# Mixer weights split in place at the mixer's end, and attention scores one slot earlier, in an early-fusion layer on one core

## The reference, cut to what matters

```python
h = s4d(log_dt, x, B, inv_A_real, A_imag, 1024)      # mixer: [16, 128, 1024]
h = concatenate([h, txt], axis=1)                    # [16, 205, 1024], txt has 77 rows

# attention, 32 heads of 32, one key head and one value head for all of them
qkv = layernorm(h) @ Wqkv                            # 1024 -> 1024 + 32 + 32
scores = einsum("bqhd,bkd->bhqk", q, k) * d ** -0.5 + alibi, causal
h = h + einsum("bhqk,bkd->bqhd", softmax(scores), v).reshape(...) @ Wo

# feed-forward: base product, and a rank-16 part of 8 experts by a router
h = h + ffn(layernorm(h))

# in the mixer, for each of 128 channels h and 64 states n
V = exp(dtA[:, :, None] * ell)                       # ell = 0 .. 1023
K = 2.0 * einsum("chn,hnl->chl", Cc, V).real
```

## Time and profile before

| what | us |
|---|---|
| median of 3 runs (1617.25 to 1621.37) | 1620.49 |
| the profiled execution: its time, its span | 1622.69, 1620.9 |
| mixer block, first instruction to the last issue of its loads | 0 to 176.4 |
| attention block until its first projection | 176.9 to 199.1 |
| pair 0; pairs 1 to 6; pair 7; drain | 59.3; 536.9; 89.6; 73.4 |
| MLP block | 958.3 to 1620.9 |

### The profile page before, as it was taken

How to read it: one execution, slowest core, us unless ns; L and a number is a source line. 1 busy time by engine, 2 the same in 40 slices (tenths; PEclk the granted TensorE clock), 3 DMA queues, 4 the chain that set the end, 5 groups by cost and what they waited for, 6 DMA issues and landing times. The chain is left out here.

```text
span 1620.9 us, 28815 instructions
## 1 busy us (share of the span) xinstructions
PE 1464.8 (90%) x9700; PEld 1312.3 (81%) x9700; DVE 1124.5 (69%) x4170; ACT 744.9 (46%) x2642; POOL 399.9 (25%) x289
## 2 busy tenths in 40 slices
PE   0477299999999999999998989999999999999999
PEld 0477298887888888887887768999898989898988
DVE  8996478889898989888888846444453544444454
ACT  4585158686878878786878731110101011110100
POOL 0000124453544445443544501101010101010110
PEclk9877699999999999999999999999999999999999
DMA  7554466465554656464567351121212121111210
GB/s 214 156 131 90 111 103 116 72 105 95 83 113 63 126 84 121 70 116 77 97 152 140 91 206 59 39 79 39 78 39 78 52 65 53 63 65 51 69 48 40
DMA packets 112269, 147.79 MB, mean 91 GB/s; under 512 B 13284, under 2 KB 97636, under 8 KB 111704
## 3 DMA queue, kind: packets, MB, share of 16 engines
q1 hardware_dynamic: 111064, 145.82, 39.5%
q10 hardware_dynamic: 1088, 0.52, 0.2%
HBM read 69.18 MB, written 46.66 MB: 71 GB/s over the span
## 5 line engine op out<-in xcount | busy, mean ns | idle before, releaser
L820 ACT ACTIVATE P<-P,nmax 128x128 f32<-128x128 f32 (+1 forms) x1024 | 434.5, 426 | 96.9 <-DVE nmax L917 93.0
L891 POOL TENSOR_TENSOR P<-P,rden 128x512 f32<-128x512 f32 (+1 forms) x256 | 329.4, 1308 | 419.8 <-DVE rden L923 419.8
L917 DVE CUSTOM_DVE_ANT_0 P<-sc,mask 128x128 f32<-128x128 f32 (+1 forms) x1024 | 292.1, 323 | 70.0 <-PE sc L695 65.3
L725 PE MATMUL pr<-xT_hi,wq_hi 128*128 128x410 f32 x576 | 242.7, 421 | 0.9 <-DVE xT_lo L943 0.9
L929 DVE COPY PTR<-pt 128x282 f32<-128x282 f32 x512 | 220.9, 432 | 17.0 <-PE pt L705 15.9
L1191 PE MATMUL b<-w_hi,x2T_hi 128*128 128x390 f32 (+3 forms) x624 | 214.7, 344 | 1.0 <-DVE x2T_lo L1323 1.0
L1191 PE MATMUL b<-w_lo,x2T_hi 128*128 128x390 f32 (+3 forms) x624 | 212.7, 341 | 0.0
L1191 PE MATMUL b<-w_hi,x2T_lo 128*128 128x390 f32 (+3 forms) x624 | 212.2, 340 | 0.0
L725 PE MATMUL pr<-xT_lo,wq_hi 128*128 128x410 f32 x576 | 201.3, 350 | 0.0
L725 PE MATMUL pr<-xT_hi,wq_lo 128*128 128x410 f32 x576 | 200.5, 348 | 0.0
L1284 POOL TENSOR_TENSOR ht<-ht 128x1024 f32<-128x1024 f32 (+1 forms) x24 | 58.3, 2428 | 575.8 <-DVE ht L1313 575.8
(11 more groups left out here) (187 smaller groups left out, 2946.0 us busy)
## 6 DMA issues: line engine op xcount, KB each, us to landing
Qs<-q_hi SPq DMA_DIRECT2D x128, 205.0 KB, 4.8
ht<-h_dram SPq DMA_DIRECT2D x42, 512.0 KB, 3.6
Qs<-q_lo SPq DMA_DIRECT2D x64, 205.0 KB, 5.7
att_dram<-att SPq DMA_DIRECT2D x64, 205.0 KB, 3.1
at<-att_dram SPq DMA_DIRECT2D x25, 512.0 KB, 4.9
out<-ht SPq DMA_DIRECT2D x23, 512.0 KB, 2.7
h_dram<-Y SPq DMA_DIRECT2D x60, 128.0 KB, 3.1
h_dram<-in_txt SPq DMA_DIRECT2D x1, 4928.0 KB, 26.0
```

Source lines behind the costliest of these rows:

```text
L725: last = nc.tensor.matmul(out, w[a][:, i, cols], xT[x][:, i, :], start=(i == 0 and m == 0), stop=(i == KC - 1 and m == 2))
L820: last = nc.scalar.activation(P[rows, j % 2, i, cols], P[rows, j % 2, i, cols], ACT.Exp, scale=-1.0, bias=nmax[at], accum_out=den[at])
L891: lastp = nc.gpsimd.tensor_tensor(w, w, r, ALU.mult)
L917: lastv = v.tensor_tensor_reduce(P[0:n, j % 2, i, cols], sc[i % 2][0:n, cols], mask[0:n, m], 1.0, 3.0e38, ALU.add, ALU.min, nmax[0:n, j % ...
```

## The change

Mixer. The stage is gone. The weights, now laid out on the host as 128 rows of nine pieces, are copied from the input to a DRAM buffer, and from there three pieces at a time into `wq_lo` itself, all issued in step 0. ACT makes pieces 0 to 4 of `wq_hi` in steps 2 to 6 and pieces 5 to 8 after the last magnitudes; DVE subtracts in place, all nine pieces after the last Q. Step 6 makes Q in quarters too, and the last step's magnitudes wait for them. SP loads the text tiles ahead of the stores of step 6, DVE norms those two tiles in the mixer block, and of the last 8 stores ACT issues 6. Attention: kv is the third projection, q2 the fourth; scores begin one slot earlier; output weights are split from slot 1 on, in turns 4 and 7; `a_lo` is done in halves; at the start DVE norms two tiles and not four; POOL fills its constant rows once they are normalized.

```diff
-    stage = sb("w_stage", [128, 2, DM])
...
+    FINE = LAST - 1
+    Q_PARTS = FINE + 2 * QUARTERS
+    SP_LAST = 2
...
-            load_piece(0)
-            load_piece(1)
-
+            sp.dma_start(io["wqkv_dram"], io["Wqkv"]).then_inc(wqkv_copied, 16)
             sp.dma_start(io["h_dram"].rearrange("(c s) d -> c s d", s=S)[:, CH:S, :], io["txt"]).then_inc(txt_copied, 16)
             for step in range(MIX_STEPS):
-                if step + 2 < PIECES:
-                    load_piece(step + 2)
+                if step == 0:
+                    sp.wait_ge(wqkv_copied, 16)
+                    for n in range(PIECES // 3):
+                        cols = slice(3 * n * DM, (3 * n + 3) * DM)
+                        sp.dma_start(W["wq_lo"][:, cols].bitcast(F32), io["wqkv_dram"][:, cols]).then_inc(w_loaded[n], 16)
...
-                if step == MIX_STEPS - 1:
-                    sp.wait_ge(q_ready, LAST + QUARTERS)
+                if step == FINE:
+                    sp.wait_ge(q_ready, Q_PARTS)
                     for c in range(2):
                         sp.dma_start(W["ht"][0:TXT, 2 * c + 1, :], io["txt"][c]).then_inc(W["h_loaded"][2 * c + 1], 16)
                 sp.wait_ge(y_copied, step + 1)
-                for a in range(AH if step < LAST else AH // 2):
+                for a in range(AH if step < LAST else SP_LAST):
...
-                    act.wait_ge(q_ready, step)
+                    act.wait_ge(q_ready, step if step < LAST else FINE + QUARTERS)
...
             for step in range(MIX_STEPS):
-                if step == LAST:
-                    hi_piece(PIECES - 1)
                 for part in ((wave, magnitudes) if step % 2 == 0 or step == LAST else (magnitudes, wave)):
                     part(step)
-                if step == 0:
-                    hi_piece(0)
-                if step < LAST:
-                    hi_piece(step + 1)
+                if 2 <= step < LAST:
+                    hi_piece(step - 2)
                 if step >= 1:
                     copy_out(step - 1)
+            for k in range(LAST - 2, PIECES):
+                hi_piece(k)
             copy_out(LAST)
...
-                lo_piece(step)
-                if step == LAST:
-                    lo_piece(PIECES - 1)
                 dve.wait_ge(wave_ready, step + 1)
-                for r in range(QUARTERS if step == LAST else 1):
+                for r in range(QUARTERS if step >= FINE else 1):
...
+            for k in range(PIECES):
+                lo_piece(k)
+
+            for c in range(2):
+                dve.wait_ge(W["h_loaded"][2 * c + 1], 16)
+                x = W["ht"][0:TXT, 2 * c + 1, :]
+                free(v.bn_stats(st[0:TXT, c, 0, :], x[:, 0:512]))
+                link(v.bn_stats(st[0:TXT, c, 1, :], x[:, 512:1024]))
+                link(v.bn_aggr(mvt[0:TXT, c, :], st[0:TXT, c].rearrange("p a b -> p (a b)")))
+            link(v.tensor_scalar(ve[0:TXT], mvt[0:TXT, :, 1], EPS, None, ALU.add))
+            for k in range(RSQRT_LINKS):
+                link(rsqrt_step(nc, k, rs[0:TXT], ve[0:TXT], rt[0:TXT]))
+            for c in range(2):
+                x = W["ht"][0:TXT, 2 * c + 1, :]
+                v.tensor_scalar(x, x, mvt[0:TXT, c, 0:1], rs[0:TXT, c:c + 1], ALU.subtract, ALU.mult).then_inc(txt_done, 1)
...
-    MAIN = [("q", 0), ("q", 1), ("q", 2), "kv", ("q", 3), ("q", 4), ("q", 5), ("q", 6), ("q", 7)]
+    MAIN = [("q", 0), ("q", 1), "kv", ("q", 2), ("q", 3), ("q", 4), ("q", 5), ("q", 6), ("q", 7)]
...
-    SCORE_SLOT = [5, 6, 7, 8, 9, 10, 11, 12]
+    SCORE_SLOT = [4, 5, 6, 7, 8, 9, 10, 11]
...
-    SPLIT_AT = [GH * (n + 2) + 2 + 3 * h for n in range(7) for h in range(2)] + [GH * SLOTS + 2 * n for n in range(4)]
+    SPLIT_AT = [GH * (n + 1) + 4 + 3 * h for n in range(WO_PIECES - 1) for h in range(2)] + [GH * SLOTS + 1, GH * SLOTS + 3]
...
-    A_HI_AT, A_LO_AT = [0, 12, 28], [1, 14, 30]
+    A_HI_AT, A_LO_AT = [0, 12, 28], [2, 14, 30]
...
             pool.wait_ge(const_loaded, 32)
+            pool.wait_ge(xn_ready, 4)
...
-            for s in (1, 3, 0, 2):
+            for s in (0, 2):
                 for part in range(3):
                     ln_stats(0, 3 * s + part, link)
             for step in range(RSQRT_LINKS + 1):
                 ln_rstd(step, link)
-            for s in range(4):
-                ln_apply(0, s, link)
+            for s in (0, 2):
+                ln_apply(0, s, link, 2)
```

More of the change, by code:

```diff
@@ L157, in mixer_block @@
     ident_loaded, txt_copied = sem("ident_loaded"), sem("txt_copied")
-    w_loaded = [sem("w_loaded0"), sem("w_loaded1")]
+    w_loaded, wqkv_copied = [sem(f"w_loaded{i}") for i in range(3)], sem("wqkv_copied")
     w_hi, w_lo = sem("w_hi"), sem("w_lo")
@@ L182, in mixer_block @@
     LAST, QUARTERS = MIX_STEPS - 1, 4
+    FINE = LAST - 1
+    Q_PARTS = FINE + 2 * QUARTERS
+    SP_LAST = 2
+    scratch = tab[:, 1].rearrange("p h a -> p (h a)")
+    st = scratch[:, 0:24].rearrange("p (c a b) -> p c a b", c=2, a=2)
+    mvt = scratch[:, 24:28].rearrange("p (c a) -> p c a", c=2)
+    rs, rt, ve = (scratch[:, 28 + 2 * i:30 + 2 * i] for i in range(3))
+    txt_done = sem("txt_done")
     with nc.Block() as block:
@@ L261, in hi_piece @@
             def hi_piece(k):
-                act.wait_ge(w_loaded[k % 2], 64 * (k // 2 + 1))
-                nc.scalar.activation(piece(W["wq_hi"], k), stage[:, k % 2, :], ACT.Copy).then_inc(w_hi, 1)
+                act.wait_ge(w_loaded[k // 3], 16)
+                nc.scalar.activation(piece(W["wq_hi"], k), piece(W["wq_lo"], k).bitcast(F32), ACT.Copy).then_inc(w_hi, 1)
             def copy_out(step):
@@ L415, in _ @@
                 pe.wait_ge(x2_ready, step + 1)
-                if step < LAST:
+                if step < FINE:
                     pe.wait_ge(q_ready, step + 1)
@@ L421, in _ @@
                     out = ps[step % 2 * BANKS_STEP + j // 4][:, j % 4, :]
-                    if step == LAST and j % 4 == 0:
-                        pe.wait_ge(q_ready, step + j // 4 + 1)
+                    if step >= FINE and j % 4 == 0:
+                        pe.wait_ge(q_ready, FINE + (step - FINE) * QUARTERS + j // 4 + 1)
                     for x, first in ((X, True), (X2, False)):
@@ L983, in ln_rstd, with ln_apply @@
                     link.issued(rsqrt_step(nc, step - 1, rstd[:], veps[:], rtmp[:]))
-            def ln_apply(p, s, link):
+            def ln_apply(p, s, link, tiles=1):
                 n = TILES[s][2]
@@ L989, in ln_apply @@
                 v.tensor_scalar(ht[0:n, s, :], ht[0:n, s, :], mv[0:n, s, 0:1], rstd[0:n, s:s + 1],
-                                ALU.subtract, ALU.mult).then_inc(xn_ready, 1)
+                                ALU.subtract, ALU.mult).then_inc(xn_ready, tiles)
             def body(p, first, last):
-                link = Chain(dve, chain, CHAINS * (p + 1) if last is False else 0, const_ready)
+                link = Chain(dve, chain, CHAINS * (p + 1) - TEXT_CHAINS if last is False else 0, const_ready)
                 for slot, main, sj, tj, aj in slots(p, first, last):
@@ L1011, in body @@
                             v.tensor_tensor(lo, half_of(wo_stage(k // 2), k % 2), hi.bitcast(F32), ALU.subtract).then_inc(wo_lo, 1)
-                        if last is None and GH * slot + i in A_LO_AT:
-                            a_lo(A_LO_AT.index(GH * slot + i))
+                        for half in range(2):
+                            if last is None and GH * slot + i - half in A_LO_AT:
+                                a_lo(A_LO_AT.index(GH * slot + i - half), half)
                         if last is None and out_half(slot, i, 1)[1] == KC - 1:
```

51 lines of the change are left out of this document (23 added, 28 removed).

## The result

The changed kernel takes 1611.53 us (1609.54 to 1613.25, 5 runs), the kernel before 1620.06 beside it on the same chip: a ratio of 0.9949, 95% interval 0.9935 to 0.9964. It is faster by 8.5 us where 19.9 were forecast, and inside the range (1588 to 1614), near its upper end.

The account below looks back on a forecast made before the run. DVE was taken to pace the mixer, and PE to be busy nearly throughout the attention slots. Mixer with stores -17.2, start of attention -6.7 and slots +4.0 gave -19.9 us, from 1620.49 to 1600.6; range 1588 to 1614.

Parts of the forecast that it names:

- the size of slot 5: Attention pairs: 7.3 us of work, but q3 lands 9.6 us after slot start, so PE waits about 2 us before slot 6.
- this meeting: Slot 4 of each pair: POOL's scaling begins just before DVE's applies, costing 0.6 us per pair, between 0 and 2.6.
- every meeting with POOL costs the rest of POOL's operation: DVE and POOL share a port pair, so a collision blocks DVE for the rest of POOL's operation, 1.3 us each.
- The rival of a clock that falls behind the wait: Clock falls in each pair near slot 5's wait, losing 3.4 us x 8 = 27: 1628 us, slower; chance 0.08.
- Slot 3: Attention pairs: a slot without scores, where DVE's backlog from slot 2 is worked off; 8.3 us.
- Pair 7: Last attention pair: no norm, and a split half in turn 6 meets DVE's slack; -1.0 us, an estimate.
- The drain: End of attention: one unit less, -4.9 us, and halves of a_lo with two splits fewer, 1.5 us; together -6.4.
- q5 and q7: Attention slots: their landings, 9.0 us in a slot of 9.5 and 9.4 in one of 11.1, stay hidden.
- the copies of the weights: Mixer: DRAM copy done by 35 us, loads by 65, needed at about 72; late-weights rival 1615 us, chance 0.08 with other mixer loss.
- the start of attention: Load of h to first projection: -6.7 us, including 4.0 us for one tiny DVE instruction that ended with POOL's cast.
- the stores': Mixer end, PE's last product to load of h: eight stores and their landing take 10.1 us against 12.2, 2.1 earlier.
- PE's last two steps: Mixer steps 6 and 7: 10.27 and 10.0 us, back to back, ending at 147.5, 15.1 us earlier than before.

Follow-up runs that it names:

- experiment 5: The changed kernel with the four applies of the next pair's norm moved from turns 38 to 41 to turns 42 to 45, behind q3's lo part: 1616.69 us.
- Experiment 3: The changed kernel with SP issuing the two DMAs of q's hi part once ACT has made it; only the third waits for DVE's lo part: 1596.10 us.
- experiment 8: Experiment 1 without POOL's wait for the four normalized tiles, so its cast stands beside DVE's layer norm again: 1596.92 us.
- experiment 2: The kernel before with only the change's three attention lists (projection order, score slots, places of the output weights' splits): 1641.20 us.
- experiment 4: The changed kernel with the norm's reciprocal root at four links a turn and the four applies early, in turns 29 to 32: 1630.70 us.
- experiment 6: Two kernels from experiment 1: first with the change's split places, 1589.70 us; second also issuing q's hi DMAs before waiting for lo, 1588.34 us.
- experiment 7: The second kernel of experiment 6 with both halves of the drain's a_lo done in one turn of DVE: 1589.10 us.
- experiment 1: The changed kernel with projection order, score slots and output weights' split places put back to those of the kernel before: 1592.19 us.

## Why the prediction went wrong, step by step

**Where it failed: the size of slot 5.** The forecast had 2.7 + 6.9 = 9.6 us from the slot's start to q3's landing, and took that sum for the slot's length. From first issue to landing it was right (6.8). Two terms were not:
- The first issue came at 3.3 instead of 2.7 us, because two of the three applies ahead of the lo part took 1.15 and 1.09 us beside POOL. The forecast saw this meeting and priced it (0.6 per pair), but at slot 4, as time lost by itself. It lay in slot 4's slack and was paid on q3's path; experiment 5 took it out of there (+2.1).
- The landing is not the end of the slot. The scores that wait are those that the last turn of slot 5 issues for slot 6, and transposes of v stand behind them: 573.67 - 572.6 = 1.1 us until the next projection. The forecast left this out.

So 9.6 + 0.6 - 0.1 + 1.1 = 11.2, within 0.1 of the measured length. Per pair, slots 2 to 6 became 49.2 us from 47.5 (+1.7), against +0.6. Experiment 3 settles the cause: with only the two hi DMAs moved ahead, the pair takes 89.7 us, which is +0.2 and better than forecast, and the kernel 1596.1. That slot 5 is 9.6 us there is no confirmation of the forecast's 9.6, which was a landing: under it the forecast had 7.3 us of work, and DVE's maxima and the transposes of v make it 9.6. The two numbers agree by luck.

The prediction's argument that every meeting with POOL costs the rest of POOL's operation, up to 1.3 us, did not hold for the applies: the one at 560.47 began 0.44 us into two POOL operations of 3.01 us together and lost 0.35 us. It held for the tiny operations of the earlier trace rows and experiment 8.

**The second failed step: the clock.** The rival of a clock that falls behind the wait had a chance of 0.08 and was treated as all pairs or none. It came in two pairs of six, at the end of a wait of 2.1 us for q3 in pair 7 (6.8 us long), and in slot 5 of pair 0 (6.8 us), there behind waits of up to 0.96 us for DVE's maxima, which experiment 3 did not remove. What it cost can be read from the same slots without it: 1.6 us each in pairs 3 and 5, 0.7 in pair 0 (68.7 against 67.9 in experiment 2), and 1.9 in pair 7 (slot 6 11.7 against 10.0 in experiment 3, slot 5 12.0 against 11.8 in experiment 2). That is some 6 us of the 15 by which the slots missed their forecast, an estimate from one execution of each kernel. Half the length of each stretch, the forecast's price, would be 10. Its share in the medians was not measured by itself; experiment 3 removed waits and lower clock in pairs 1 to 7 together, 16.3 us by the traces, and that is the price of both. Experiments 4 and 5 show how large the clock's share can get when waits for DVE are added. That an identical wait of about 1.3 us is followed by the lower level in pair 3 and not in pair 4 stays open.

**Other terms.** Slot 3 was forecast 8.3 and is 9.6: PE waits 0.9 us for copies in its middle, behind a link that took 1.06 us. These 1.3 us are nearly as much as slot 5's 1.5; slots 2, 4 and 6 won 0.2, 0.7 and 0.2 back. Pair 7 was given -1.0; without the wait and the lost clock it is -2.8 (86.9 in experiment 3), and experiment 6 shows that the split's places alone give -3.6. The drain gave 5.1 of 6.4, since the halves of `a_lo`, counted as help, put the second one beside POOL; but repairing that (experiment 7) won nothing clear of the clock, so the missing 1.3 us stay open.

**Where it was right.** q5 and q7 stayed hidden, as worked out; so did the copies of the weights (text copy landed 37.2 us from its issue against 26.0 before, and still nothing waited). In the start of attention it was -7.0 against -6.7; the 4 us given to POOL's wait came back as 4.7 in experiment 8, though by another operation than before the change. In the mixer DVE's times were met within 0.2 us (Q's last quarter ends at 137.6; text norm at 154.5 against 154.3), and the stores' -2.0 against -2.1 is right only in sum: the six DMAs and their landing took 8.2 us against 10.1, but ACT's four late pieces pushed the first issue to 2.7 us behind PE's last product, where 0.7 had been assumed. The forecast named these pieces and gave them no price. And what it read as agreement in ACT's four DMAs (4.63 us where SP's pace gives 2.7) shows only that ACT's issue takes longer; no run moved the stores from one engine to the other.

**Where it was mis-sized to the good.** PE's last two steps were priced at 20.3 us by rows that held half-clock stretches; at 1.00 they take 14.5. That is 5.7 us, almost the whole surplus of the front part (-29.8 for -23.9).

The version that beats both kernels keeps the mixer part and the split's places and puts order and score slots back: 1588.3 us with the hi DMAs first, 1589.7 without, which the runs do not tell apart.

## What to carry to other kernels

When a change shortens the time between a producer and its consumer, follow the new deadline to the first instruction of the next slot, not to the landing: what the engine still has to do behind the wait is paid too, and so is everything that now stands ahead of the producer on its own engine. A split "hi and lo" operand need not be sent as one: issuing the part that is ready 1.9 us earlier took 16 us of waits and lower clock out of the pairs here. And before a duration is taken from a row, its clock has to be read: the same 64 products took 7.3, 8.75 and 10.3 us.

## What the runs showed of the hardware that was not expected

- Stretches at the lower clock of 3.4 and 6.8 us began within about 1.5 us of the end of a wait of 1.0 to 2.1 us; PE had been busy 1.74 of the 3.0 us before one of them. Of the same waits of 1.3 to 1.5 us in six pairs two did so in one execution and four of six in another (experiment 2).
- Tiny DVE operations on 128x4 values beside POOL took 0.89 to 5.57 us instead of 0.16; also an apply of 0.80 took 1.54, and a subtraction of 0.6 to 0.7 took 2.04, ending 0.5 us behind POOL's.
- In the traces of experiments 3, 4, 5, 7 and of the second kernel of experiment 6, h was loaded at 150.7 to 151.7 us; in those of the changed kernel, of experiments 1 and 8 and of the first kernel of experiment 6 at 152.4 to 152.7, although nothing of the mixer differs. It is not the hi DMAs, since experiments 4 and 5 leave them as they were. It goes with the clock in PE's step 5: its 64 products took 8.9 to 9.0 us in the first group and 10.1 to 10.3 in the second, ACT's four late pieces began at 137.2 to 137.5 and not at 138.4 to 138.7, and its first store at 143.1 to 143.3 and not at 144.3 to 144.5. PE's last product ended at 141.7 to 141.9 in all, so ACT and not PE set the mixer's end. The few tenths that are left lie in the stores and stay open.
